# Moving one copy on ScalarE from step 7 to step 1 of the next batch, and writing a loop out

## The chip, the cores and the metric

The kernel runs on one core of a Trainium2 chip. The core has a matrix engine (TensorE, PE in the profile), a vector engine (VectorE, DVE), an activation engine (ScalarE, ACT), a general engine (GpSimd, POOL) and SyncE (SP), which here only issues DMAs. Each runs its own instruction stream; they meet only at semaphores. The metric is the device time of one execution in microseconds (us), the median of several.

## The reference, cut to what matters

The input is 8 images of 32x32 positions with 128 channels: 8 sequences of 1024 tokens. Three blocks follow each other.

```python
q = (x * dw1 @ pw1 + b1);  v = (x * dw2 @ pw2 + b2)          # per image, 1024 x 128
t = softmax(q @ q.T) @ v * gamma + x                         # attention inside an image
t = t + ssm(layernorm(t))                                    # conv, gated state-space scan
n = layernorm(t)                                             # the normed rows
probs = softmax(n @ router_w.T)                              # 8 experts
gates, experts = top_k(probs, 2)                             # a first and a second choice
out = t + sum(gate * expert(n) for both choices)
```

## The kernel before, in words

A **tile** is 128 tokens; there are 64, and a **batch** is the 8 tiles of one image (`NT` = 8). The program has two stages. In the first, which this change touches, all of attention, scan, norm and routing are done tile by tile, and every token's normed row is written to DRAM twice, once for each choice, into a region of its expert (`rows_by_expert`). In the second, 136 groups of 128 rows are fetched from there, run through their expert and written back; then the results are added and stored.

The first stage is a software pipeline written out by hand. Every engine has a function `step(base, i)` and runs it through `batches(eng, step)` (L191) 79 times: `base` is the first tile of a **round** (0, 8, 16, ..., 72) and `i` the step in it, 0 to 7. I number rounds by base / 8, so rounds 0 to 9. In step `i` of a round the engines work on several tiles at once: the scores of tile `base + i`, the rest of attention for the tile before it, the scan five and six tiles back, and the routing of the *batch before*, or of the one before that. The order in an engine's stream is the order of the lines of its `step`; what must wait for another engine does so by `upto(eng, semaphore, base, c)`. Rounds 0 and 1 are written out, rounds 2 to 6 are one loop with register `base` (`Fori`, L196), and rounds 7 to 9 are written out again. In the rounds of the loop a semaphore is compared with a value worked out in a register.

The path of one batch's normed rows, for the batch before round r:

- ScalarE, step 6 of round r (L657 to L665): writes the 8 normed tiles to `XA[:, 0]`, after it has waited for `scattered0`, the writes to DRAM of the previous content for the first choice.
- TensorE and ScalarE, step 7: `rows_of_x` (L303, L678) turns the rows, `logits` (L314) multiplies with the router.
- ScalarE, step 7 (L635 to L638): copies `XA[:, 0]` to `XA[:, 1]`, the rows for the second choice, in one instruction of 128x1024. It waits for `scattered1`: the eight writes of `XA[:, 1]`'s previous content. Behind it in ScalarE's stream stand `take_q` (L564, the next image's `QH`), the evacuation of the scan's projection (`XBC`, L646 and L648), and the first tap of the convolution (`CV`, L653). Who waits for them: `take_ql` on VectorE, the scores and the transposes `pY` (L334) on TensorE, and VectorE's convolution (L954).
- VectorE, step 1 of round r + 1: `route_a` (L889), the top two experts and gates, after a wait for `xa_copied`. Step 3: `route_b` (L923), the row numbers `SL`.
- GpSimd, steps 3 to 7 of round r + 1: one indirect DMA per tile and choice (`scatter_rows`, L863), issued at places named in the table `SPREAD` (L769). Rows 0 to 7 are the first choice, rows 8 to 15 the second; 8 to 11 stand in step 6 and 12 to 15 in step 7, at places 0 to 3. The last of them, row 15, is issued at place 3 of step 7.

In the last round (9) no tile is computed any more; its steps only route and write the last batch.

Of the kernel before, what the change touches and what calls it, by code (L numbers as in the profile page):

```python
# [5 lines left out]
def conv_attn_ssm_moe(nc, x, xT, dw1, pw1, b1, dw2, pw2, b2, gamma, w_zdt, w_xbc, conv_w, conv_b,  # L6
                      dt_bias, a_log, d_skip, gnorm_w, norm_w, w_outT, routerT, w1T, w3T, w2T, out):
    fp32, bf16, f32r = mybir.dt.float32, mybir.dt.bfloat16, mybir.dt.float32r
    ALU, ACT, AX = mybir.AluOpType, mybir.ActivationFunctionType, mybir.AxisListType
    P = 128  # L10
    TILES = x.shape[0] // P
    NT = 8
    SEQ = NT * P
    C = x.shape[1]
# [18 lines left out]
    with ctx:  # L33
        def sb(name, shape, dt=fp32):
            return ctx.enter_context(nc.sbuf_tensor(name, shape, dt))
# [4 lines left out]
        def sem(name):  # L40
            return ctx.enter_context(nc.semaphore(name))
# [61 lines left out]
        XA = sb("XA", [P, TOP, NT, ROW])  # L103
# [50 lines left out]
        def s(name):  # L154
            if name not in S:
                S[name] = sem(name)
            return S[name]

        def upto(eng, name, base, c):

            if not isinstance(base, int):
                eng.wait_ge(s(name), base + c)
            elif base + c > 0:
                eng.wait_ge(s(name), min(base + c, TILES))

        def apart(eng):

            eng.sem_inc(s("apart"), 1)

        class Steps:  # L170
# [5 lines left out]
            def then(self, ins, last=False):  # L176
                self.n += 1
                assert self.n < self.total
                if last:
                    ins.then_inc(self.sem, self.total - self.n + 1)  # L180
                    self.n = self.total
                else:
                    ins.then_inc(self.sem, 1)
                self.eng.wait_ge(self.sem, self.start + self.n)

        def there(base, c):
            return not isinstance(base, int) or 0 <= base + c < TILES
# [3 lines left out]
        def batches(eng, step):  # L191


            for i in range(2 * NT):
                step(i // NT * NT, i % NT)
            with eng.Fori(2 * NT, TILES - 2 * NT + 1, NT) as base:  # L196
                for i in range(NT):
                    step(base, i)
            for i in range(3 * NT - 1):
                step(TILES - NT + i // NT * NT, i % NT)  # L200

        NLOAD = 2 + 3 + 2 + 3 + 3 + 2 + 1 + 1

# [84 lines left out]
        def _(pe):  # L288
# [201 lines left out]
            project_q()  # L490
            pe.wait_ge(s("consts"), 1)
            batches(pe, step)


# [60 lines left out]
        def _(act):  # L555
            A = nc.scalar.activation
# [10 lines left out]
            def step(base, i):  # L567
# [63 lines left out]
                    last.then_inc(s("tr_ready"), 2)  # L631
                if i == 7 and there(base, -NT):
                    rows_of_x(base, 1)

                    upto(act, "xa_ready", base, 0)  # L635
                    if not (isinstance(base, int) and base == NT):
                        act.wait_ge(s("scattered1"), base * 16 - 16 * NT)
                    A(XA[:, 1, :, 0:C], XA[:, 0, :, 0:C], ACT.Copy).then_inc(s("xa_copied"), NT)  # L638
                if i == NT - 1 and there(base, NT):
                    upto(act, "qps", base, 2 * NT)  # L640
                    upto(act, "s_ready", base, NT)
# [32 lines left out]
                if i == 0 and there(base, -2 * NT):  # L674
                    upto(act, "lsub_ready", base, -NT)
                    A(PB[:], LG[:], ACT.Exp).then_inc(s("pexp_ready"), NT)

            def rows_of_x(base, grp):  # L678
                upto(act, "vT_ps", base, 4 * grp - 4)
                A(VT[:], pd[:], ACT.Copy).then_inc(s("vT_ready"), 4)  # L680
# [3 lines left out]
            act.wait_ge(s("loaded"), 16 * NLOAD)  # L684
            A(hrow[:, 1, :], hrow[:, 1, :], ACT.Exp).then_inc(s("a_exp"), 1)
            batches(act, step)

            def rows_T(n, par):
# [41 lines left out]
        def _(pool):  # L730
# [133 lines left out]

            pool.wait_ge(s("loaded"), 16 * NLOAD)
            batches(pool, step)

            def put(t, j):
# [9 lines left out]
        def _(dve):  # L878
# [10 lines left out]
            def route_a(base):  # L889

                bc = lambda a: a[:, :, None].broadcast_to([P, NT, E])
                steps = Steps(dve, "route_a_steps", base, -2 * NT, NT, 4)
                then = steps.then

                upto(dve, "xa_copied", base, -NT)
                v.tensor_copy(XA[:, 0, :, C + 1], TOK[:])
                ts(XA[:, 1, :, C + 1], TOK[:], float(TOKENS), None, ALU.add)
                upto(dve, "pexp_ready", base, -NT)
                then(v.tensor_reduce(r8[:, 1, :], PB[:], AX.X, ALU.add))
                then(v.reciprocal(r8[:, 2, :], r8[:, 1, :]))  # L900
                then(ts(TOK[:], TOK[:], float(NT * P), None, ALU.add))
                then(tt(PB[:], PB[:], bc(r8[:, 2, :]), ALU.mult))
                apart(dve)
                for j in range(NT):
                    last = v.max(M8[:, j, :], PB[:, j, :])
                then(last)
                apart(dve)
                for j in range(NT):
                    last = v.max_index(IX[:, j, :], M8[:, j, :], PB[:, j, :])
                then(last)  # L910
                then(tt(r8[:, 3, :], M8[:, :, 0], M8[:, :, 1], ALU.add))
                then(ts(r8[:, 4, :], r8[:, 3, :], 1e-9, None, ALU.add))
                then(v.reciprocal(r8[:, 5, :], r8[:, 4, :]))
                for c_ in range(TOP):
                    last = tt(XA[:, c_, :, C], M8[:, :, c_], r8[:, 5, :], ALU.mult)
                last.then_inc(s("xb_ready"), NT)
                then(v.tensor_copy(IXF[:], IX[:, :, 0:TOP]))
                for c_ in range(TOP):
                    last = tt(OH[:, c_], iota8[:, None, :].broadcast_to([P, NT, E]), bc(IXF[:, :, c_]), ALU.is_equal)
                then(last, True)  # L920
                tt(OHS[:], OH[:, 0], OH[:, 1], ALU.add).then_inc(s("onehot_ready"), NT)
# [17 lines left out]
            def step(base, i):  # L939
# [78 lines left out]
                if i == 1 and there(base, -2 * NT):  # L1018
                    route_a(base)
# [228 lines left out]
```

## Time and profile before

| | us |
|---|---|
| median of 3 runs | 1347.85 |
| lowest, highest | 1344.8, 1347.96 |
| the profiled execution | 1343.85 |
| its span (first to last instruction) | 1342.0 |
| first stage: until the first group's rows are fetched | about 978 |
| second stage | about 364 |
| one round of the loop | 111.2 |

The profile is of one execution. Its busy shares (TensorE 85%, VectorE 68%, ScalarE 51%, GpSimd 45%) are averages of both stages. The time between two rounds is best read from one event that every round has once: ScalarE's copy `V<-pX` (L669) in step 0, or VectorE's maximum over the scores `NM<-pX` (L980), which every step has once. In the timelines, "[3.73 <-DMA ...]" after a row is the time for which the engine sat idle before it, and what ended that; a row without it followed its predecessor at once.

### The profile page before, as it was taken

The numbers are of one execution on the slowest core, as the hardware profiler recorded it, in microseconds if no ns is written. First come the engines' busy times: TensorE is split into PE (matmuls) and PEld (weight loads), VectorE is DVE, ScalarE is ACT, GpSimd is POOL, SyncE is SP. The second block draws the span as 40 slices with busy tenths as digits, with TensorE's granted clock in tenths as the row PEclk, the third lists the DMA queues.
The fourth block names the chain that finished last, engine by engine and source line by source line (L and its number), as shares of the span: only waits on it lengthen the run. The fifth ranks groups of instructions, "written<-read, shape, count | busy, mean of one in ns | idle before, by whom it ended". The sixth has DMA issues, their size and how long they took to land.

```text
span 1342.0 us, 28912 instructions
## 1 busy us (share of the span) xinstructions
PE 1135.7 (85%) x7681; PEld 955.2 (71%) x7745; DVE 908.2 (68%) x3041; ACT 689.9 (51%) x1748; POOL 604.5 (45%) x846
## 2 busy tenths in 40 slices
PE   4799999998998998998999899774079999999950
PEld 3688888787877787877787787663058888888740
DVE  2578778867986886986898798672535555555535
ACT  2565675566565666566656666542034444444420
POOL 4133334573473465357347437436424444444430
PEclk9899999999999999999999999987579999999985
DMA  6000000100010010010001100000112222222239
GB/s 176 25 1 9 25 2 9 35 23 9 4 44 16 0 40 17 8 36 20 9 6 42 33 6 17 13 1 31 44 47 58 57 59 57 59 57 59 57 106 302
DMA packets 73005, 54.26 MB, mean 40 GB/s; under 512 B 9781, under 2 KB 67677, under 8 KB 72925
## 3 DMA queue, kind: packets, MB, share of 16 engines
q1 hardware_dynamic: 55437, 31.62, 8.7%
q0 software_dynamic: 8448, 17.45, 3.9%
q10 hardware_dynamic: 9040, 4.33, 1.1%
q8 instruction: 26, 0.43, 0.1%
q14 instruction: 54, 0.44, 0.1%
HBM read 30.67 MB, written 22.69 MB: 40 GB/s over the span
## 4 chain that ended last, share of the span: by engine, by line
PE 32%; DVE 19%; POOL 14%; issue 13%; DMA 4%; ACT 3%; DVEq 1%; SPq 1%; POOLq 0%; ACTq 0%
POOL rows_by_expert L863 7%; PE pX L512 6%; PE pY L514 6%; PE pd L529 3%; PE pb L529 3%; PE pc L521 3%; DVE CV L954 3%; PE pc L367 2%; DVE NM L980 1%; DMA rows_by_expert<-XA,SL 1%; POOL st L853 1%; PE pa L501 1%; PE pa L428 1%; DVE OFF L930 1%; POOL YG L810 1%
## 5 line engine op out<-in xcount | busy, mean ns | idle before, releaser
L872 POOL DMA_INDIRECT results_by_choice<-YE,DIX x136 | 130.2, 957 | 191.5 <-ACT YE L703 182.2
L863 POOL DMA_INDIRECT rows_by_expert<-XA,SL x128 | 139.5, 1090 | 64.1 <-issue 32.6
L1180 DVE COPY V<-pc 128x384 f32<-128x384 f32 x136 | 75.8, 558 | 133.3 <-PE pc L521 132.4
L367 PEld LDWEIGHTS pc<-XDT,M 128*128 128x128 f32 x1024 | 125.4, 196 | 35.9 <-issue 30.2
L367 PE MATMUL pc<-XDT,M 128*128 128x64 f32 x1024 | 126.3, 278 | 23.4 <-DVE CT L1085 9.8
L954 DVE SCALAR_TENSOR_TENSOR CV<-XBC,cw,CV 128x256 f32<-128x256 f32 x288 | 131.2, 491 | 20.7 <-issue 9.6
L428 PE MATMUL pa<-V,PT 128*128 128x128 f32 x1024 | 126.6, 277 | 2.2 <-POOL V L860 0.9
L428 PEld LDWEIGHTS pa<-V,PT 128*128 128x128 f32 x1024 | 119.4, 192 | 5.8 <-issue 5.3
L512 PE MATMUL pX<-W,TA 128*128 x272 | 104.7, 466 | 1.0 <-ACT TA L690 0.7
L810 POOL TENSOR_TENSOR YG<-Y,SZ 128x256 f32<-128x256 f32 x64 | 46.5, 727 | 123.0 <-DVE Y L1001 112.8
L514 PE MATMUL pY<-W,TA 128*128 x272 | 101.7, 456 | 0.0
L1045 DVE TENSOR_TENSOR M<-ED,GT 128x1024 f32<-128x1024 f32 x64 | 78.3, 1223 | 32.8 <-ACT ED L627 31.9
L801 POOL TENSOR_TENSOR STE<-ST,ETOT 32x256 f32<-32x256 f32 x56 | 46.5, 831 | 106.7 <-DVE ST L1102 102.6
L1176 DVE TENSOR_TENSOR X<-XT,pY 128x341 f32<-128x341 f32 x136 | 69.5, 511 | 31.7 <-PE pY L514 19.8
L980 DVE TENSOR_REDUCE NM<-pX 128x1 f32<-128x1024 f32 x64 | 77.9, 1217 | 14.2 <-PE pX L346 14.1
L334 PE MATMUL pY<-ident,PR 128*128 128x128 f32 x512 | 70.7, 283 | 19.5 <-ACT XBC L648 18.7
L673 ACT ACTIVATE TH<-CV 128x768 f32<-128x768 f32 x32 | 27.0, 844 | 112.3 <-issue 100.6
L334 PEld LDWEIGHTS pY<-ident,PR 128*128 128x128 f32 x512 | 59.7, 150 | 28.6 <-issue 15.2
L690 ACT ACTIVATE TA<-pa 128x128 f32<-128x128 f32 x136 | 37.7, 277 | 81.4 <-PE pa L501 80.6
L615 ACT ACTIVATE PR<-pX,NM 128x1024 f32<-128x1024 f32 x64 | 71.2, 1113 | 9.4 <-DVE NM L980 9.4
L521 PE MATMUL pc<-ident,X 128*128 128x128 f32 (+1 forms) x408 | 67.2, 274 | 0.0
L584 ACT ACTIVATE PT<-pY 128x1024 f32<-128x1024 f32 x64 | 64.4, 1006 | 3.8 <-PE pY L334 3.8
(252 smaller groups left out, 3022.0 us busy)
## 6 DMA issues: line engine op xcount, KB each, us to landing
GX<-rows_by_expert SPq DMA_DIRECT2D x136, 65.0 KB
XT<-in_xT_dram SPq DMA_DIRECT2D x8, 512.0 KB, 4.4
X<-in_x_dram SPq DMA_DIRECT2D x16, 256.0 KB, 2.9
W<-results_by_choice SPq DMA_DIRECT2D x8, 512.0 KB, 8.6
out_dram<-T ACTq DMA_DIRECT2D x8, 512.0 KB, 6.9
results_by_choice<-YE,DIX POOLq DMA_INDIRECT x136, 2.2
rows_by_expert<-XA,SL POOLq DMA_INDIRECT x128
W<-in_w1T_dram SPq DMA_DIRECT2D x1, 1364.0 KB
```

The source lines that it names most:

```text
L334: last = nc.tensor.transpose(pY[:, P * j:P * j + P], PR[:, P * j:P * j + P], ident[:])
L367: mm(pc[:, 64 * h:64 * h + 64], M[:, h, :], XDT[:, e % 2, HD * h:HD * h + 64], start=h == 0, stop=False, skip_group_check=True)
L428: last = mm(pa[:, 0:C], PT[:, P * j:P * j + P], V[:, j, :], start=j == 0, stop=j == NT - 1)
L512: mm(pX[:, 512 * par:512 * par + HID], GXT[:, par, :], W1[:, cols], start=True, stop=True).then_inc(s("h1_ps"), 1)
L514: mm(pY[:, 512 * par:512 * par + HID], GXT[:, par, :], W3[:, cols], start=True, stop=True).then_inc(s("h3_ps"), 1)
L521: last = nc.tensor.transpose(pc[0:hn, P * k:P * k + P], HH[:, par, h0:h0 + hn], ident[:])
L529: last = mm((pd, pb)[par][:, 0:C], HT[0:hn, par, k, :], W2[0:hn, bass.ds(expert, 1), k, :], start=k == 0, stop=k == len(HC) - 1)
L863: g.indirect_dma_start(xg, bass.IndirectOffsetOnAxis(ap=SL[:, j // NT, j % NT:j % NT + 1], axis=0), XA[:, j // NT, j % NT, :], None).then_ ...
L872: g.indirect_dma_start(yg, bass.IndirectOffsetOnAxis(ap=DIX[:, j, :], axis=0), YE[:, j, :], None).then_inc(s(f"ye{j}_scattered"), 16)
L954: return stt(CV[:, m, :], XBC[:, m, fo + tap:fo + tap + 256], cw[:, m, tap:tap + 1], CV[:, m, :], ALU.mult, ALU.add)
L980: v.tensor_reduce(NM[:, i:i + 1], pX[:], AX.X, ALU.max, negate=True).then_inc(s("nm_ready"), 1)
L1045: tt(M[:], ED[:], GT[:, None, :].broadcast_to([P, H, P]), ALU.mult).then_inc(s("m_ready"), 1)
```

## The change

The copy for the second choice leaves step 7 of ScalarE and stands at the end of step 1 of the next round. Its wait for `scattered1` asks for the same batch's writes as before (the base has grown by 8, so 8 tiles' worth is subtracted more). `route_a` on VectorE, which writes two columns of `XA[:, 1]`, waits for `scattered1` itself, in place of `xa_copied`. GpSimd still waits for `xa_copied` before row 0 in step 3. The table `SPREAD`, which puts the second choice's rows into steps 6 and 7, is the same in both files. `batches` becomes one written-out sequence of 79 steps on each of the four engines, so `base` is always a number.

```diff
         def batches(eng, step):
-            for i in range(2 * NT):
+            for i in range(TILES + 2 * NT - 1):
                 step(i // NT * NT, i % NT)
-            with eng.Fori(2 * NT, TILES - 2 * NT + 1, NT) as base:
-                for i in range(NT):
-                    step(base, i)
-            for i in range(3 * NT - 1):
-                step(TILES - NT + i // NT * NT, i % NT)
...
                 if i == 7 and there(base, -NT):
                     rows_of_x(base, 1)
-
-                    upto(act, "xa_ready", base, 0)
-                    if not (isinstance(base, int) and base == NT):
-                        act.wait_ge(s("scattered1"), base * 16 - 16 * NT)
-                    A(XA[:, 1, :, 0:C], XA[:, 0, :, 0:C], ACT.Copy).then_inc(s("xa_copied"), NT)
...
+                if i == 1 and there(base, -2 * NT):
+                    upto(act, "xa_ready", base, -NT)
+                    if not (isinstance(base, int) and base == 2 * NT):
+                        act.wait_ge(s("scattered1"), base * 16 - 32 * NT)
+                    A(XA[:, 1, :, 0:C], XA[:, 0, :, 0:C], ACT.Copy).then_inc(s("xa_copied"), NT)
...
-                upto(dve, "xa_copied", base, -NT)
+                if not (isinstance(base, int) and base == 2 * NT):
+                    dve.wait_ge(s("scattered1"), base * 16 - 32 * NT)
```

ScalarE, end of step 7 of a loop round and the first instructions of the next round, before (`VT` is the turned rows for the router, `QH` the next image's q, `PT` the transposed weights of the softmax, `TZ` the gate):

```order
L680 ACTIVATE VT<-pd 128x512 [waits vT_ps]
L638 ACTIVATE XA<-XA 128x8x128 [waits scattered1,xa_ready]
L162 REGISTER_ALU
L564 ACTIVATE QH<-pX,pcol 128x512 [waits s_ready,qps]
L564 ACTIVATE QH<-pX,pcol 128x512
L646 ACTIVATE XBC<-pc 128x2x256 [waits xbc01_ps]
L648 ACTIVATE XBC<-pY 128x256 [waits xbc2_ps]
L653 ACTIVATE CV<-XBC,cb,cw 128x256 [waits sx_ready,xbc2_evac]
L653 ACTIVATE CV<-XBC,cb,cw 128x256 x2
L196 REGISTER_ALU
L196 COMPARE_AND_BRANCH
```

The same place in the changed kernel (its lines have other numbers):

```order
L675 ACTIVATE VT<-pd 128x512 [waits vT_ps]
L559 ACTIVATE QH<-pX,pcol 128x512 [waits s_ready,qps]
L559 ACTIVATE QH<-pX,pcol 128x512
L636 ACTIVATE XBC<-pc 128x2x256 [waits xbc01_ps]
L638 ACTIVATE XBC<-pY 128x256 [waits xbc2_ps]
L643 ACTIVATE CV<-XBC,cb,cw 128x256 [waits sx_ready,xbc2_evac]
L643 ACTIVATE CV<-XBC,cb,cw 128x256 x2
L579 ACTIVATE PT<-pY 128x1024 [waits o_ps,pT_ps]
```

The copy and the branch are gone from there. ScalarE, end of step 1 and start of step 2 of the changed kernel:

```order
L636 ACTIVATE XBC<-pc 128x2x256 [waits xbc01_ps]
L638 ACTIVATE XBC<-pY 128x256 [waits xbc2_ps]
L643 ACTIVATE CV<-XBC,cb,cw 128x256 [waits sx_ready,xbc2_evac]
L643 ACTIVATE CV<-XBC,cb,cw 128x256 x2
L671 ACTIVATE XA<-XA 128x8x128 [waits scattered1,xa_ready]
L579 ACTIVATE PT<-pY 128x1024 [waits o_ps,pT_ps]
L595 ACTIVATE TZ<-pb 128x256 [waits sz_ready,z_ps]
L595 ACTIVATE TZ<-pd 128x256 [waits sz_ready,z_ps]
```

The copy now stands between the third convolution start and step 2's `PT`. VectorE, the end of a loop round and the start of the next one, before (`LG` the logits less their maximum, `CV` the convolution):

```order
L1102 TENSOR_TENSOR ST<-STE,pd 32x256 [waits ste_ready]
L1109 TENSOR_REDUCE r<-LG 128x8 [waits lg_ready]
L1111 TENSOR_TENSOR LG<-LG,r 128x64 [waits lmax_ready]
L196 REGISTER_ALU
L196 COMPARE_AND_BRANCH
L954 SCALAR_TENSOR_TENSOR CV<-XBC,cw,CV 128x256 [waits cv01_evac]
L954 SCALAR_TENSOR_TENSOR CV<-XBC,cw,CV 128x256
L954 SCALAR_TENSOR_TENSOR CV<-XBC,cw,CV 128x256 [waits cv_evac]
L980 TENSOR_REDUCE NM<-pX 128x1 [waits s_ready]
```

The same place in the changed kernel:

```order
L1098 TENSOR_TENSOR ST<-STE,pd 32x256 [waits ste_ready]
L1105 TENSOR_REDUCE r<-LG 128x8 [waits lg_ready]
L1107 TENSOR_TENSOR LG<-LG,r 128x64 [waits lmax_ready]
L950 SCALAR_TENSOR_TENSOR CV<-XBC,cw,CV 128x256 [waits cv01_evac]
L950 SCALAR_TENSOR_TENSOR CV<-XBC,cw,CV 128x256
L950 SCALAR_TENSOR_TENSOR CV<-XBC,cw,CV 128x256 [waits cv_evac]
```

The instructions that do work are the same and in the same order; the two that close the loop are gone.

## Rows read from the trace of the kernel before

**Rows 1.** Page, chain that ended last, share of the span by engine

```profile
PE 32%; DVE 19%; POOL 14%; issue 13%; DMA 4%; ACT 3%; DVEq 1%; SPq 1%; POOLq 0%; ACTq 0%
```

**Rows 2.** Waits: engine, line, waited for; us in total, times, longest

```profile
ACT XA L638 <- DMA rows_by_expert<-XA,SL: 25.2, 7, 4.0
```

**Rows 3.** Timeline, round 2 to 3: start us, us, engine, line, instruction

```profile
296.88 0.60 ACT L680 ACTIVATE VT<-pd 128x512 f32<-128x512 f32 x1 [0.55 <-PE pd L311]
298.80 0.96 POOL L863 DMA_INDIRECT rows_by_expert<-XA,SL  x1 [0.30 <-issue]
300.95 0.59 PE L472 MATMUL pd<-XW,BNAT 128*128 128x256 f32 x2
301.20 1.06 ACT L638 ACTIVATE XA<-XA 128x1024 f32<-128x1024 f32 x1 [3.73 <-DMA rows_by_expert<-XA,SL]
304.23 1.96 PE L334 MATMUL pY<-ident,PR 128*128 128x128 f32 x8 [2.68 <-ACT XBC L648]
305.80 0.62 DVE L1111 TENSOR_TENSOR LG<-LG,r 128x64 f32<-128x64 f32 x1
308.83 1.28 DVE L954 SCALAR_TENSOR_TENSOR CV<-XBC,cw,CV 128x256 f32<-128x256 f32 x3 [2.40 <-issue]
310.02 1.22 DVE L980 TENSOR_REDUCE NM<-pX 128x1 f32<-128x1024 f32 x1
```

**Rows 4.** Timeline, round 1 to 2, the entry into the loop

```profile
191.28 0.60 ACT L680 ACTIVATE VT<-pd 128x512 f32<-128x512 f32 x1 [0.54 <-PE pd L311]
191.78 1.05 ACT L638 ACTIVATE XA<-XA 128x1024 f32<-128x1024 f32 x1
195.79 1.04 PE L334 MATMUL pY<-ident,PR 128*128 128x128 f32 x8
198.78 1.22 DVE L980 TENSOR_REDUCE NM<-pX 128x1 f32<-128x1024 f32 x1
```

**Rows 5.** Timeline, round 6 to 7, the exit from the loop

```profile
741.76 0.60 ACT L680 ACTIVATE VT<-pd 128x512 f32<-128x512 f32 x1 [0.56 <-PE pd L311]
751.15 1.26 DVE L954 SCALAR_TENSOR_TENSOR CV<-XBC,cw,CV 128x256 f32<-128x256 f32 x3
752.34 1.21 DVE L980 TENSOR_REDUCE NM<-pX 128x1 f32<-128x1024 f32 x1
```

**Rows 6.** Timeline of ScalarE, step 0 to step 7, rounds 6 and 7

```profile
652.74 1.02 ACT L669 ACTIVATE V<-pX 128x1024 f32<-128x1024 f32 x1 [2.77 <-PE pX L300]
736.60 0.58 ACT L680 ACTIVATE VT<-pd 128x512 f32<-128x512 f32 x1
761.38 1.02 ACT L669 ACTIVATE V<-pX 128x1024 f32<-128x1024 f32 x1 [2.90 <-PE pX L300]
845.22 0.58 ACT L680 ACTIVATE VT<-pd 128x512 f32<-128x512 f32 x1
```

**Rows 7.** Timeline of TensorE, round 7 to 8

```profile
853.74 0.59 PE L472 MATMUL pd<-XW,BNAT 128*128 128x256 f32 x2
856.89 1.63 PE L334 MATMUL pY<-ident,PR 128*128 128x128 f32 x8 [2.55 <-ACT XBC L648]
```

**Rows 8.** Timeline of VectorE, round 8 to 9

```profile
941.37 0.23 DVE L1111 TENSOR_TENSOR LG<-LG,r 128x64 f32<-128x64 f32 x1
942.42 0.21 DVE L899 TENSOR_REDUCE r<-PB 128x8 f32<-128x64 f32 x1
```

**Rows 9.** Timeline of ScalarE, start of step 2 in round 2

```profile
223.47 1.00 ACT L584 ACTIVATE PT<-pY 128x1024 f32<-128x1024 f32 x1
225.03 0.38 ACT L600 ACTIVATE TZ<-pb 128x256 f32<-128x256 f32 x1 [0.55 <-PE pb L352]
225.75 0.38 ACT L600 ACTIVATE TZ<-pd 128x256 f32<-128x256 f32 x1 [0.34 <-PE pd L355]
```

**Rows 10.** DMA queues, 319 to 430 us: packets, MB, share of 16 engines

```profile
q14 instruction: 6, 0.05, 0.1%
```

**Rows 11.** DMA queues, 761 to 845 us, the same columns

```profile
q8 instruction: 5, 0.08, 0.5%
```

## The prediction

> **What bounds the kernel now.** I read the page first, then the waits, then timelines around the places that the waits name. The page's chain changes hands all the time: TensorE 32% of the span, VectorE 19%, GpSimd 14%, and 13% in which an engine waited for nothing the profile shows [rows 1]. So no engine is the bound; in the first stage the end is set by hand-overs, and a wait counts where it stands in that chain. Among the waits one belongs to the moved copy: ScalarE stood 25.2 us before it, in 7 rounds, until DMA writes of rows had landed [rows 2]. Those are rounds 2 to 8; round 1 has no earlier writes.
>
> The timeline of round 2 shows what that costs [rows 3]. ScalarE has the turned logit rows `VT` at 296.88 and then stands 3.73 us until the write issued at 298.80 has landed; the copy starts at 301.20 and takes 1.06. TensorE is through with its step at 301.5 (300.95 + 0.59) and stands 2.68 us until 304.23, for `XBC`, which is queued behind the copy. So this wait is on the path. Then a second hole: VectorE ends `LG` at 306.42 and starts the next round's `CV` only at 308.83, after 2.40 us marked issue, and the maximum `NM` of the new round follows at 310.02. From `VT` to `NM` it is 13.14 us.
>
> Two other boundaries show the same instructions without one or both holes. Round 1 to 2 has no writes to wait for: the copy starts at once at 191.78, the transposes at 195.79 without idle time, and from `VT` to `NM` it is 198.78 - 191.28 = 7.50 us [rows 4]. Round 6 to 7 has the writes but leaves the loop without jumping back: `CV` follows at 751.15 without idle time, and `VT` to `NM` is 752.34 - 741.76 = 10.58 us [rows 5]. So the wait for the writes costs 10.58 - 7.50 = 3.08 us, and the jump back costs 13.14 - 10.58 = 2.56 us, which is the 2.40 us hole and a little around it.
>
> **The change, part by part.**
>
> *The copy leaves step 7.* With it goes the wait. What is late next is known from round 1: there the copy itself (1.05 us) stood in ScalarE's stream and TensorE still ran on without idle time [rows 4], so the boundary is then TensorE's own row of products followed by VectorE's `LG` and `CV`. Taking out the copy's own 1.05 us therefore gives nothing in round 1, and nothing beyond the 7.50 us in the others. Rounds 2 to 6: 5 x 3.08 = 15.4 us. Round 7 computes no next image, so I read it from TensorE alone: its products end at 854.33 and the transposes start at 856.89, 2.55 us idle for `XBC` [rows 7]: 2.6 us. Round 8 has only routing left: VectorE's `LG` is done at 941.60 and `route_a`'s first sum starts at 942.42 [rows 8], with the end of the copy and the exponential between them. Without the copy in front of the exponential about 0.5 us of those 0.82 goes. Sum: 15.4 + 2.6 + 0.5 = 18.5 us.
>
> *The loop is written out.* The jump back is taken 4 times (rounds 2 to 3, 3 to 4, 4 to 5, 5 to 6): 4 x 2.56 = 10.2 us. Inside a round nothing is to be had: from `V` in step 0 to the first `VT` in step 7 the loop's round 6 takes 736.60 - 652.74 = 83.86 us and the written-out round 7 takes 845.22 - 761.38 = 83.84 us [rows 6]. The register arithmetic before the waits is hidden. The same pair bounds what straight code costs: round 7 runs it once and never again, and is no slower. Its price is more code to fetch: a loop round has 6 instruction packets on q14 and none on q8 [rows 10], the straight round has 5 on q8 in 84 us [rows 11]. I take 0 for it; what it costs if the cover is gone is a rival below.
>
> The Trainium skill (Advanced Engine Details and Errata, Control Flow Timing) gives a compare-and-branch about 108 ns. By that figure alone the four jumps would be worth 0.4 us and the whole change 18.9 us instead of 28.7. The trace does not agree with it as the whole cost of a jump: 2.40 us stand there on VectorE in the loop, none at the exit. The same page (ISA Cache) says that an engine's instruction cache holds two lines of 256 instructions, four times as much on TensorE, so a jump far back lands outside it; that would fit a jump that costs more than its own execution, but no row here shows it directly.
>
> *The copy arrives in step 1, in rounds 2 to 9.* It is 1.06 us on ScalarE, after the third `CV` and before step 2's `PT`. In round 2 `PT` starts at 223.47, ends at 224.47, and ScalarE then stands 0.55 us for TensorE before the first `TZ` and 0.34 us before the second at 225.75 [rows 9]. With the copy `PT` ends at 225.5, the first `TZ` starts at 225.5 instead of 225.03, and the second at about 225.8: the two holes, 0.89 us, swallow it but for some 0.1 us, and VectorE takes up `TZ` only after its `NM` of the step. `PT` itself is needed by products that stand at the end of TensorE's step. I take 0; the upper end is 8 x 1.06 = 8.5 us, the lower 0, since nothing leaves step 1. Its wait for the writes is over: the last write landed by 301.2, before the new round's first `NM`, and step 2 starts some 25 us after that `NM` (223.47 - 198.78 in round 2) [rows 3, 4, 9]. Behind the wait stand `PT` and `TZ`, should it not be.
>
> *The waits of the others.* VectorE's new wait for the same writes has the same answer. GpSimd waits for `xa_copied` in step 3, a full step after the copy. No DMA is added, removed or issued earlier in the order; the last writes of step 7 now overlap with products and transposes that before stood behind them. They touch nothing the engines use then.
>
> **The sum.** 18.5 + 10.2 = 28.7 us. The profiled execution took 1343.85 us (span 1342.0), so it would be 1315.2. The median of the runs shown, 1347.85, lies 4.0 above that execution; the same saving gives 1319.2, and that is what I forecast: **1319 us**.
>
> **The rivals.**
>
> *A: the hole at the jump does not go* (10%). The 2.40 us are marked issue, so the profile names no cause. If it belongs to the boundary and not to the jump, it stays; against that speaks the exit from the loop, with the same writes and no hole [rows 5]. It would leave 18.5 us: 1347.85 - 18.5 = 1329 us. By the Trainium skill's figure for a branch (Advanced Engine Details and Errata, Control Flow Timing) it would be 1329 us too.
>
> *B: something takes the wait's place* (8%). Round 1, my model, has no row writes on GpSimd in step 7, the others have. If they make the norm and state work late, each boundary gives back a part; half of the 15.4 is 7.7 us. The copy could also be on the path in step 1 after all, 8.5 us. Either alone: 1327 to 1328 us; both: 1335 us. Against it: up to `VT` and the products that follow, round 2 keeps round 1's pace: the last product starts 4.07 us after `VT` (300.95 - 296.88) and ends at 4.66, and in round 1 the transposes behind it start at 4.51 [rows 3, 4].
>
> *C: slower, because straight code has to be fetched* (4%). The mechanism: in rounds 2 to 6 TensorE's code came from its cache; now about 6 more packets a round come through q8. Their share, 0.5% of 16 DMA engines over 84 us, is 6.7 us or 1.3 us for one [rows 11]. If all 30 stood open they would cost 40 us, against a gain of 28.7: 1347.85 + 11 = 1359 us. It decides from some 22 of the 30 unhidden. Against it: round 7 fetches the same way and loses nothing [rows 6]. It would have to be that five such rounds in a row are unlike one.
>
> *D: more than forecast* (8%). Where TensorE has stood before, its next group is long: the eight transposes take 1.96 us at the jump and 1.63 us in round 7, against 1.04 in round 1 [rows 3, 4, 7]. In round 7 up to 0.6 us of that may come back, and later steps may gain a little likewise: up to 5 us in all, 1314 us.
>
> **How the numbers follow.** Forecast 70%, A 10%, B 8%, C 4%, D 8%. The forecast's own spread is small, about 4 us to each side, since the profiled execution and the median are 4 us apart. The range from 1312 to 1330 holds the forecast, A, D and the mild half of B. A measurement of this kernel can tell 0.3%, 4 us, from no change. Faster by more than that: forecast, A, B and D less 0.01 for a B far worse than priced, 0.95; C's 0.04 is split by how many fetches stand open: within 0.3% with the 0.01, 0.02; slower 0.03.
>
> **What would show it.** In the changed kernel's profile: no idle time of ScalarE before the copy; the copy in step 1 right after `CV`; `VT` to `NM` at about 7.5 us at every boundary of rounds 1 to 7 and no issue hole before `CV`; rounds of 105.5 us instead of 111.2; transposes of round 8 right after the products of round 7; about 30 more packets on q8. A hole before `CV` would mean A; 7.9 us or more between `VT` and `NM`, or a first `TZ` that VectorE waits for, B; idle time marked issue on TensorE in the middle of steps, C.

## The result, and the profile after

The changed kernel takes 1314.16 us in the median of 4 runs (1313.46 to 1316.24), the kernel before 1346.32 in 4 runs (1344.47 to 1347.96). The ratio is 0.9764, 95% interval 0.9744 to 0.9784: 31.8 us faster, with 29.1 to 34.5 as the ends of the interval. The forecast was 1319, a saving of 28.7. The profiled execution took 1313.46 us, its span is 1311.5 (1342.0 before).

Timeline of the changed kernel, round 2 to 3 (the place of [rows 3]), all engines, some rows:

```profile
295.58 0.60 ACT L675 ACTIVATE VT<-pd 128x512 f32<-128x512 f32 x1 [0.54 <-PE pd L306]
...
299.66 0.59 PE L467 MATMUL pd<-XW,BNAT 128*128 128x256 f32 x2
...
300.09 1.05 PE L329 MATMUL pY<-ident,PR 128*128 128x128 f32 x8
...
301.21 0.40 PE L340 MATMUL pX<-QL,QH 128*128 128x512 f32 x1
...
301.33 0.55 DVE L1107 TENSOR_TENSOR LG<-LG,r 128x64 f32<-128x64 f32 x1
...
301.80 1.27 DVE L950 SCALAR_TENSOR_TENSOR CV<-XBC,cw,CV 128x256 f32<-128x256 f32 x3
302.99 1.21 DVE L976 TENSOR_REDUCE NM<-pX 128x1 f32<-128x1024 f32 x1
```

Both holes are gone. The transposes start at 300.09 with no idle time named, in place of 2.68 us for `XBC`; `CV` follows `LG` at once, in place of 2.40 us of issue. From `VT` to `NM` it is 302.99 - 295.58 = 7.41 us instead of 13.14, and it is 7.41 at each boundary of rounds 2 to 6. The transposes take 1.05 us instead of 1.96.

ScalarE of the changed kernel, end of step 1 of round 2, where the copy now stands (compare [rows 9]):

```profile
220.79 0.59 ACT L643 ACTIVATE CV<-XBC,cb,cw 128x256 f32<-128x256 f32 x1
221.29 1.05 ACT L671 ACTIVATE XA<-XA 128x1024 f32<-128x1024 f32 x1
222.24 1.00 ACT L579 ACTIVATE PT<-pY 128x1024 f32<-128x1024 f32 x1
223.14 0.36 ACT L595 ACTIVATE TZ<-pb 128x256 f32<-128x256 f32 x1
224.14 0.38 ACT L595 ACTIVATE TZ<-pd 128x256 f32<-128x256 f32 x1 [0.64 <-PE pd L350]
```

The copy starts at once and `TZ` still waits for TensorE afterwards. Among the waits of the changed kernel none stands before the copy; the 25.2 us of [rows 2] are gone.

`V<-pX` in step 0 dates the rounds. The changed kernel, rounds 2 to 5:

```profile
205.89 1.03 ACT L659 ACTIVATE V<-pX 128x1024 f32<-128x1024 f32 x1 [2.66 <-PE pX L295]
...
312.03 1.02 ACT L659 ACTIVATE V<-pX 128x1024 f32<-128x1024 f32 x1 [2.67 <-PE pX L295]
...
417.48 1.02 ACT L659 ACTIVATE V<-pX 128x1024 f32<-128x1024 f32 x1 [2.67 <-PE pX L295]
...
523.48 1.02 ACT L659 ACTIVATE V<-pX 128x1024 f32<-128x1024 f32 x1 [2.67 <-PE pX L295]
```

A round takes 106.1, 105.5 and 106.0 us instead of 111.2. The whole difference of the spans, 30.5 us, lies as follows, worked out from such rows of both traces:

| stretch | saved, us | forecast |
|---|---|---|
| start, until the first `QH` (15.59 before, 13.65 after) | 1.9 | 0 |
| `V` of round 2 to `V` of round 7 (553.51, 529.01) | 24.5 | 25.6 |
| second `VT` of round 7 to that of round 8 (87.65, 84.34) | 3.3 | 2.6 |
| after that | 1.1 | 0.5 |

(`VT` is written in two halves; the second is the one shown at 295.58.) In the second line the forecast is 4 jumps and 5 waits, 4 x 2.56 + 5 x 3.08 = 25.6; 1.1 less was saved: the five boundaries gave 26.2, and the rounds between them lost 1.7 (below). The rows add to 30.8; the 0.3 left is above all the inside of round 7, from `V` to the second `VT`, where the change lost 0.4 us (89.36 against 88.99). The first line is not the change's: `before` issued its first loads at the same time, but its first products start at 11.77 us instead of 9.83, and every other kernel timed here has its first `QH` between 13.3 and 13.8. Less it, the two profiles differ by 28.6 us.

### The profile page after: what moved, and what is told of

The parts are those of the page before. It is cut to its first block and busy times, and to the rows that moved or that the text cites. A ratio compares the mean times of both kernels' runs of the same rounds, so it can differ in the third digit from the quotient of the medians.

```text
span 1311.5 us, 28238 instructions
## 1 busy us (share of the span) xinstructions
PE 1128.5 (86%) x7681; PEld 949.8 (72%) x7745; DVE 908.1 (69%) x3041; ACT 689.1 (53%) x1748; POOL 603.7 (46%) x846
## 5 line engine op out<-in xcount | busy, mean ns | idle before, releaser
L524 PEld LDWEIGHTS pb<-W,V 128*128 128x128 f32 (+1 forms) x408 | 56.1, 191 | 14.0 <-issue 1.1
```

What stands on the lines that cost most here:

```text
L524: last = mm((pd, pb)[par][:, 0:C], HT[0:hn, par, k, :], W2[0:hn, bass.ds(expert, 1), k, :], start=k == 0, stop=k == len(HC) - 1)
```

## The experiments

All eight timed kernels ran in two groups, each beside its own runs of the kernel before (7 in each; medians 1344.27 in the first group, 1343.22 in the second). Ratios are against those, with 95% intervals.

**One part alone.** `copy_only` moves the copy and leaves the loop standing, but over rounds 3 to 6 only, so with 3 jumps back and not 4 (in round 2 the new wait has no writes to ask for, and must know that when it is built). `unroll_only` writes the loop out and leaves the copy and its wait in step 7.

```diff
 copy_only, against the kernel before: the copy moved as in the change, and
-            for i in range(2 * NT):
+            for i in range(3 * NT):
                 step(i // NT * NT, i % NT)
-            with eng.Fori(2 * NT, TILES - 2 * NT + 1, NT) as base:
+            with eng.Fori(3 * NT, TILES - 2 * NT + 1, NT) as base:
 unroll_only, against the kernel before:
-            for i in range(2 * NT):
+            for i in range(TILES + 2 * NT - 1):
                 step(i // NT * NT, i % NT)
-            with eng.Fori(2 * NT, TILES - 2 * NT + 1, NT) as base:
-                for i in range(NT):
-                    step(base, i)
-            for i in range(3 * NT - 1):
-                step(TILES - NT + i // NT * NT, i % NT)
```

> The copy is moved to step 1 as in the change, but the loop stays, over rounds 3 to 6 (rounds 0 to 2 and 7 to 9 written out), so the jump back is taken 3 times instead of 4. My theory, two separate costs at a boundary: the wait goes (18.5 us) and one of four jumps goes (2.6 us): 21 us below before, about 1325 us, and 2.56 us too much at each of the three jumps, with a hole marked issue on VectorE before CV. The rival, that the hole before CV is a consequence of the stall on ScalarE and not of the jump: no hole at any boundary, and the time of the changed kernel, about 1314 us.

> The copy stays in step 7 with its wait; only the loop is written out. My theory: the four jumps go, 10.2 us below before, about 1336 us; ScalarE still stands 3.7 us before the copy in rounds 2 to 8. From VT to NM 10.6 us at every boundary of rounds 2 to 6. The rival, that the hole hangs on the stall: 2.4 us stay before CV and the time stays near before's, 1346 us. Inside the rounds: the changed kernel needed 89.0 to 89.7 us from V to the second VT where before had 89.0; if that is from straight code, it is here too; if it is from the copy in step 1, it is not.

Measured: `copy_only` 1323.97 us, ratio 0.9862 (0.9829 to 0.9896); `unroll_only` 1334.72 us, ratio 0.9927 (0.99 to 0.9954). By the ratios that is 18.6 us saved (14.0 to 23.0) and 9.8 (6.2 to 13.4), so each part is a gain alone; the two forecasts of a saving were 21 and 10.2. That `copy_only` came so near its forecast time of 1325 is in part luck: the saving was 2.4 us smaller, and the kernel before was faster in this group. The change has both parts. `copy_only`, round 3 to 4, VectorE's rows and TensorE's a few us later:

```profile
409.49 1.28 DVE L955 SCALAR_TENSOR_TENSOR CV<-XBC,cw,CV 128x256 f32<-128x256 f32 x3 [2.41 <-issue]
410.69 1.22 DVE L981 TENSOR_REDUCE NM<-pX 128x1 f32<-128x1024 f32 x1
...
415.21 0.43 PE L408 MATMUL pb<-ident,YG 128*128 128x128 f32 x2 [2.59 <-POOL YG L810]
415.48 3.17 PE L428 MATMUL pa<-V,PT 128*128 128x128 f32 x16
```

The hole at the jump stays, 2.41 us of issue, though the copy and its wait are gone. `VT` is at 400.71 there, so to `NM` it is 9.98 us, 2.57 above the change's 7.41: the jump's own price as forecast. But `V` comes at 421.38, 20.67 after `VT`, against 312.03 - 295.58 = 16.45 in the change: 4.2 us. The other 1.6 are TensorE's. It stood 2.59 us before 415.21, and its group of 16 products then took 3.17 us; the same group takes 1.95 us elsewhere in the kernel before (at 425.97). One stretch of `copy_only`, columns: us, then busy us and instructions of PE, PEld, DVE, ACT and POOL, then TensorE's granted clock as a share of the full one:

```profile
415.00:419.00 4.00, 3.79 (x21) 3.80 (x22) 3.68 (x15) 1.79 (x4) 1.50 (x4) 0.62 0.00 0
```

The clock was 0.62 there, so mostly at the lower of its two levels, 1.2 instead of 2.4 GHz. `unroll_only` has the mirror image, round 2 to 3:

```profile
299.56 1.06 ACT L633 ACTIVATE XA<-XA 128x1024 f32<-128x1024 f32 x1 [3.80 <-DMA rows_by_expert<-XA,SL]
...
302.68 1.94 PE L329 MATMUL pY<-ident,PR 128*128 128x128 f32 x8 [2.84 <-ACT XBC L643]
...
304.62 1.26 DVE L949 SCALAR_TENSOR_TENSOR CV<-XBC,cw,CV 128x256 f32<-128x256 f32 x3
...
304.84 0.63 PE L340 MATMUL pX<-QL,QH 128*128 128x512 f32 x1
```

The wait stands, the issue hole before `CV` is gone. TensorE stood 2.84 us, the transposes take 1.94 and a product of the scores 0.63, where the change shows 1.05 and 0.40. So the new round's `NM` is late too: from `VT` to `NM` it is 12.05, 11.21, 11.41, 10.81 and 11.22 us at the five boundaries, where I had expected 10.6 at each. TensorE's granted clock, and that of the kernel before and the change at the same place, in this order:

```profile
303.00:307.00 4.00, 4.00 (x15) 3.42 (x14) 2.79 (x9) 2.17 (x4) 0.61 (x1) 0.50 0.02 4
```

```profile
304.00:308.00 4.00, 3.77 (x14) 3.34 (x15) 2.32 (x7) 2.78 (x5) 0.61 (x1) 0.57 0.01 4
```

```profile
300.00:305.00 5.00, 5.00 (x37) 4.56 (x35) 4.60 (x13) 3.23 (x6) 0.61 (x1) 1.00 0.01 3
```

So in these three places, where TensorE had stood for 2.6 to 2.8 us, the products behind it ran at 0.50 to 0.62 of its clock; in the change it doesn't fall there. Two boundaries of one trace show what the clock alone does. In `dve_loop` (next experiment) TensorE stood 2.42 us before 415.11 and 2.35 us before 523.56, at two successive jumps without the wait, and ran its group of 16 products at a clock of 1.00 (415 to 419 us) and of 0.67 (524 to 528 us):

```profile
415.83 2.02 PE L432 MATMUL pa<-V,PT 128*128 128x128 f32 x16 [0.28 <-issue]
...
524.28 3.16 PE L432 MATMUL pa<-V,PT 128*128 128x128 f32 x16
```

From `VT` to `V` it is 19.42 us at the first and 20.48 at the second, 3.0 and 4.0 above the change: of the 4.2 us, the low clock is some 1.1, and standing alone did not bring it every time. What the other 0.4 us beyond the hole's 2.6 are is open. In the kernel before that slow stretch lay under VectorE's hole: much of TensorE's slow work ran while VectorE stood in a hole of its own. With one hole gone, the other brings its slow stretch onto the path; that reading fits the rows, but no run held the clock fixed. By the distance from `VT` to `V`, the two prices are (means over the five boundaries of the change and of `unroll_only`, the three jumps of `copy_only` and the four of the kernel before; `unroll_only` alone ranges from 19.85 to 22.18):

| `VT` to `V`, us | no wait | wait |
|---|---|---|
| no jump | 16.45 | 20.81 |
| jump | 20.63 | 22.21 |

The wait alone costs 4.4, the jump alone 4.2, both 5.8, not 8.5. My forecast split its 5.64 into 3.08 and 2.56; the total holds, since the change undoes both.

**Which engine's jump.** Both kernels have the moved copy. In `dve_straight` VectorE's stream is written out and TensorE, ScalarE and GpSimd loop over rounds 3 to 6; in `dve_loop` VectorE alone loops.

```diff
 dve_straight, in batches, before the loop of copy_only:
+            if eng in (nc.vector,):
+                for i in range(TILES + 2 * NT - 1):
+                    step(i // NT * NT, i % NT)
+                return
 dve_loop, there:
+            if eng in (nc.scalar, nc.gpsimd, nc.tensor,):
+                for i in range(TILES + 2 * NT - 1):
+                    step(i // NT * NT, i % NT)
+                return
```

> The changed kernel, but TensorE, ScalarE and GpSimd run a loop over rounds 3 to 6; VectorE alone is written out. If the jump costs time only on VectorE, the time is that of the changed kernel, 1314 to 1317 us. If the other engines' jumps count as well (before, the transposes took 1.96 instead of 1.04 us at a jump), 0.8 to 2.5 us more at each of 3 jumps: 1317 to 1322 us.

> The mirror image: VectorE alone runs the loop over rounds 3 to 6, the other three are written out. If VectorE's own jump is the cost: 3 x 2.56 = 7.7 us above the changed kernel, about 1322 us, with the hole before CV. If it takes all engines jumping at once (for instance if they share what brings the code): less than half of that, 1314 to 1318 us.

Measured: `dve_straight` 1313.48 us, ratio 0.9769 (0.9746 to 0.9793), as fast as the change; `dve_loop` 1328.79 us, ratio 0.9884 (0.986 to 0.9909). First two rows of `dve_straight`, then two of `dve_loop`, round 3 to 4:

```profile
399.31 0.60 ACT L684 ACTIVATE VT<-pd 128x512 f32<-128x512 f32 x1 [0.58 <-PE pd L315]
...
406.80 1.21 DVE L985 TENSOR_REDUCE NM<-pX 128x1 f32<-128x1024 f32 x1
```

```profile
409.63 1.28 DVE L959 SCALAR_TENSOR_TENSOR CV<-XBC,cw,CV 128x256 f32<-128x256 f32 x3 [2.58 <-issue]
410.82 1.22 DVE L985 TENSOR_REDUCE NM<-pX 128x1 f32<-128x1024 f32 x1
```

Three engines jump in `dve_straight` and `VT` to `NM` is 7.49 us; VectorE alone jumps in `dve_loop` (`VT` at 400.75) and it is 10.07. All of the jump's price is VectorE's. The expectation for `dve_loop` was too low by some 7 us: by `VT` to `V` its three jumps cost 3.0, 4.0 and 4.0 us, 11.1 and not 3 x 2.56 = 7.7, and its round 7 to 8 took 90.3 us, 5.9 more than the change's, in the profiled execution (below).

**Where the copy may stand.** `copy_twice` writes the same rows a second time to a scratch tile `XC` in step 1, in rounds 2 to 9. `copy_step2` puts the one copy into step 2, in front of `TH`. `copy_end7` puts it last in step 7, behind `QH`, `XBC` and `CV`. `changed_again` is the changed kernel itself, run beside them.

```diff
 copy_twice, against the change, ahead of the copy in step 1:
+                    if base > 2 * NT:
+                        act.wait_ge(s("extra"), base // NT - 2)
+                    for k_ in range(1):
+                        last = A(XC[:, k_], XA[:, 0, :, 0:C], ACT.Copy)
+                    last.then_inc(s("extra"), 1)
 copy_end7, against the change, last in ScalarE's step:
+                if i == 7 and there(base, -NT):
+                    upto(act, "xa_ready", base, 0)
+                    if not (isinstance(base, int) and base == NT):
+                        act.wait_ge(s("scattered1"), base * 16 - 16 * NT)
+                    A(XA[:, 1, :, 0:C], XA[:, 0, :, 0:C], ACT.Copy).then_inc(s("xa_copied"), NT)
-                if i == 1 and there(base, -2 * NT):
...
```

> The changed kernel itself once more, beside the variants of this call, since they differ from it by a few us at most. Expected 0.976 of before, within the first measurement's interval of 0.9744 to 0.9784.

> The changed kernel with a second copy of the same rows (into a scratch tile) in front of the first in step 1; it costs ScalarE 8 x 1.06 us more. If step 1 has the slack that I read from the two holes (0.89 us) and the one copy fits in, the second one must show: PT another 1.0 us later, the second TZ up to 1 us late, and 0 to 1 us a round, 0 to 8 us in all. The rival, that ScalarE in steps 1 and 2 is far from the path since VectorE's NM comes first: no change, under 2 us.

> The changed kernel with the copy in step 2, in front of TH, where ScalarE stood 5.3 us idle in every round. If the copy in step 1 costs anything (the excess of 0.1 to 0.7 us inside each round of the changed kernel), it comes back here, up to 2 us; if that excess is VectorE's straight code, as the run with only the loop written out says, the time is the changed kernel's within 1 us.

> The changed kernel with the copy back in step 7, but as ScalarE's last instruction there, behind QH, XBC and CV. What stalled before was what stood behind the waiting copy; the last write lands 4.3 us after VT and CV ends 6 us after VT, so the copy waits for nothing here. My theory: nearly all of the gain stays; PT of the next step 0 starts about 1 us later and TZ by up to 0.5 us, so 0 to 0.5 us for each of 5 boundaries, at most 3 us above the changed kernel. The rival, that the writes and the copy disturb the boundary by being there at all (contention): 5 us or more above.

| kernel | median, us | ratio | 95% interval |
|---|---|---|---|
| changed_again | 1314.80 | 0.9790 | 0.9767 to 0.9813 |
| copy_twice | 1316.23 | 0.9801 | 0.9776 to 0.9825 |
| copy_step2 | 1315.24 | 0.9791 | 0.9769 to 0.9814 |
| copy_end7 | 1315.15 | 0.9783 | 0.9760 to 0.9806 |

None can be told from the change. `changed_again` has the time of the change, 1314.80 for 1314.16 us, but its ratio of 0.9790 lies just outside the 0.9744 to 0.9784 that I had expected it in: the kernel before took 1343.22 us beside it and 1346.32 beside the first measurement. ScalarE of `copy_twice`, round 2, step 1 to 2:

```profile
221.13 1.05 ACT L675 ACTIVATE XC<-XA 128x1024 f32<-128x1024 f32 x1
222.09 1.04 ACT L677 ACTIVATE XA<-XA 128x1024 f32<-128x1024 f32 x1
223.03 1.00 ACT L580 ACTIVATE PT<-pY 128x1024 f32<-128x1024 f32 x1
223.94 0.36 ACT L596 ACTIVATE TZ<-pb 128x256 f32<-128x256 f32 x1
224.20 0.37 ACT L596 ACTIVATE TZ<-pd 128x256 f32<-128x256 f32 x1
```

The second copy uses up the rest of the holes before `TZ`, both of which are gone, and the rounds inside stay within 0.05 us of the change, but for one at 0.2. The second `TZ` comes at 224.20 where the change has 224.14; I had allowed it up to 1 us, so the two holes were not all the room there is, and of the two expectations it is the rival, under 2 us, that holds. Step 1 has room for two copies, and the 0 that I took for one is not luck. ScalarE of `copy_end7`, round 2 to 3:

```profile
297.21 1.27 ACT L559 ACTIVATE QH<-pX,pcol 128x512 fp32r<-128x512 f32 x2 [1.06 <-PE pX L289]
299.02 0.60 ACT L636 ACTIVATE XBC<-pc 128x512 f32<-128x512 f32 x1 [0.55 <-PE pc L450]
...
301.42 1.05 ACT L668 ACTIVATE XA<-XA 128x1024 f32<-128x1024 f32 x1
```

The copy is still in step 7 and its wait too, but by 301.42 the writes have landed, and no idle time stands before it. What cost time was neither the copy nor its step: it was that `QH`, `XBC` and `CV` were queued behind a waiting instruction. With these in front, the wait is over when it is reached.

**What makes VectorE's jump dear.** Two probes add, behind the last addition of the changed kernel, loops of 4 turns on VectorE whose bodies are n small copies (128x1) to a scratch tile. Each turn waits on a semaphore that the turn before raised. Nothing of the output is left out; the extra work makes the whole time long, and it is only the holes that are read.

```diff
+            dve.sem_inc(s("turned"), 1)
+            for k, n in enumerate((256, 320, 340, 360, 380, 400, 420)):
+                with dve.Fori(0, 4, 1) as turn:
+                    dve.wait_ge(s("turned"), turn + 4 * k + 1)
+                    for j in range(n):
+                        last = v.tensor_copy(probe[:, j:j + 1], pcol[:, 0:1])
+                    last.then_inc(s("turned"), 1)
```

`jump_probe` has the bodies 16, 64, 110, 150, 220, 300 and 420 in their place.

> The changed kernel with seven small loops on VectorE behind its last addition, each of 4 turns over a body of 16, 64, 110, 150, 220, 300 or 420 copies of 128x1; they touch only a scratch tile and run while the results are stored or after it. At each of 21 jumps the hole before the first copy of the next turn is read. VectorE's loop in the kernel before had 353 instructions and a hole of 2.4 us. Theory: the cost of a jump depends on how far back it goes; under 0.5 us for 16 and 64, about 2 us or more for 300 and 420, with a step in between. Rival: a jump costs VectorE 2.4 us whatever the body (then the probe shows it for 16 as well). Second rival: far jumps are cheap too and the 2.4 us belonged to the place (then no hole over 0.5 us anywhere).

> The same probe with bodies of 256, 320, 340, 360, 380, 400 and 420 copies. The first one had no hole up to 300 and one of 2.2 us, with a second of 1.5 to 1.8 us 11 copies later, at 420. If what counts is whether the whole body stays in what the engine holds of its code, there is one length between 300 and 420 from which every jump has a hole of 2.2 us, and below which none has, and VectorE's 353 instructions of the kernel before lie above it or within some tens of it (where a body starts may shift it). If instead the hole grows with the length, it is between 0 and 2.2 us for 340 to 400.

Measured: `jump_probe` 1638.45 us, with no hole at any jump of a body up to 300, where I had expected about 2 us at 300, and 2.2 to 2.3 us at each jump of the 420, with a second hole of 1.5 to 1.8 us 11 copies later. `jump_probe2` 1948.68 us: no hole at 256 and 320, one of 2.2 to 2.5 us at each jump from 340 on, and no second one at its 420. `jump_probe2`, a stretch of one turn of the 320 and one of the 340:

```profile
1392.05:1411.53 19.48, 0.00 (x0) 0.00 (x0) 19.45 (x323) 0.00 (x0) 0.00 (x0) 0.50 0.00 0
1494.36:1517.24 22.88, 0.00 (x0) 0.00 (x0) 20.66 (x343) 0.00 (x0) 0.00 (x0) 0.50 0.01 2
```

The first is busy for 19.45 of 19.48 us, the second has 2.2 us in which nothing runs. What ends the hole, on the timeline, and the DMA queues from 1517.3 to 1520.2:

```profile
1520.09 1.00 DVE L1209 COPY probe<-pcol 128x1 f32<-128x1 f32 x15 [2.22 <-issue]
```

```profile
q14 instruction: 1, 0.01, 1.1%
```

One packet of instructions arrives in the hole, and nothing else; the same queue has one packet in the hole of the kernel before (306 to 309 us), and none at a jump of the 320. So the engine jumps back to code that it no longer holds, and waits until it is fetched.

What it holds is not told by the length alone. A packet of this queue is 8 KB, and `dve_straight` tells how much code that is: from 410 us on VectorE alone runs straight code there, and between the first and the last of the eleven packets from 410 to 719 us VectorE's trace has 1283 instructions, waits on semaphores included: 128 for each of ten packets. The packets of that stretch, then those of the first turn of the 320 and of the 340 in `jump_probe2`:

```profile
q14 instruction: 11, 0.09, 0.1%
```

```profile
q14 instruction: 2, 0.02, 0.3%
```

```profile
q14 instruction: 3, 0.02, 0.5%
```

The code comes in pieces of 128, then, and the first turn of a body brings one packet for each new piece that it runs into: two for the 320, three for every body from 340 to 420, and four for the 420 of `jump_probe`, the one with the second hole, which starts at another place in a piece:

```profile
1552.63 24.84 DVE L1209 COPY probe<-pcol 128x1 f32<-128x1 f32 x409 [1.47 <-issue]
```

This second hole stands 11 copies behind the jump. In both probes the next packet starts some 0.5 us behind the first hole (1550.92 us here); a body that starts near the end of a piece wants that code before it is there, which is how I read the second hole. The other 420, like the 340, has none. So 340 and 420 cost the same, and 420 costs more at one start than at another: the start in a piece counts as well as the length. One end stays open: the 256 has three packets as well, the first right at its start and the last 0.06 us before its first branch, and no hole. The limit between 320 and 340 holds for these starts only; no other length than 420 was run at two. VectorE's loop in the kernel before is well beyond it: from branch to branch its trace has 515 instructions, 305 that work and 210 on registers, branches and semaphores, not the 353 of my expectations. ScalarE's has 273.

In the Trainium skill (Advanced Engine Details and Errata, ISA Cache) an engine holds two lines of 256 instructions. A loop of 515 is too long for that, as the trace agrees, but the probe does not agree with the size: the first turns of the 340 and the 360 run into six pieces in a row, so one of the two bodies would lie in no more than two lines of 256, and both have the hole at each jump.

## Why the prediction was right

*The two holes and what is late next: right.* Round 1 to 2 was the right model: 7.41 us at each boundary, forecast 7.50. Rival A is refuted (no issue before `CV`), and B too: the writes on GpSimd delay nothing by then, and the copy in step 1 is free, with room for another (`copy_twice`).

*The split into 3.08 and 2.56: wrong as prices, right as a sum.* The first came from a boundary without a jump against one without either, the second from subtraction, so that the sum is 13.14 - 7.50 whatever they are. Alone they are worth 4.4 and 4.2 at `V`. I read both off at `NM`, and so missed that TensorE, slow after having stood, is late with the next step's products. For the wait it shows at `NM` already: without jumps it cost 3.4 to 4.6 us there in `unroll_only`, not 3.08. Of the exit in the kernel before, round 6 to 7, `VT` to `V` is 19.62 us (761.38 - 741.76, [rows 5, 6]): 3.17 above 16.45, where the same wait in `unroll_only` costs 4.4 in the mean. Why the exit is milder is open.

*Straight code at no cost: a little wrong.* Round 2, VectorE's maxima of two steps, of the kernel before (loop) and of the change (straight):

```profile
251.31 1.21 DVE L980 TENSOR_REDUCE NM<-pX 128x1 f32<-128x1024 f32 x1
265.37 1.23 DVE L980 TENSOR_REDUCE NM<-pX 128x1 f32<-128x1024 f32 x1
```

```profile
249.71 1.20 DVE L976 TENSOR_REDUCE NM<-pX 128x1 f32<-128x1024 f32 x1
264.11 1.22 DVE L976 TENSOR_REDUCE NM<-pX 128x1 f32<-128x1024 f32 x1
```

The step takes 14.40 us instead of 14.06. There are such losses of about 0.35 us at a few fixed places, at the same ones when the change ran again; from `V` to `VT` rounds 2 to 7 lose 2.1 us in all (89.69, 89.0, 89.54, 89.4, 89.12 and 89.36, against 89.0). `unroll_only` and `dve_straight`, whose VectorE is straight too, have them, and in the rounds that VectorE loops in `copy_only` they are missing (88.7 to 89.1). That it is code fetched for VectorE fits this, and in the change a packet of q14 follows 0.7 us behind three such places (222.43, 252.18 and 468.03 us), but it was not measured by itself. So the rounds take 105.5 to 106.1 us and not 105.5 as I had put down. My comparison of rounds 6 and 7 in the kernel before [rows 6] was of two rounds that happened to agree. Of rival C, fetches on TensorE, there is nothing: q8 has 24 packets more than before, about the 30 forecast, and they cost nothing that the times show. The page of the change, then of the kernel before:

```profile
q8 instruction: 50, 0.82, 0.3%
```

```profile
q8 instruction: 26, 0.43, 0.1%
```

*Round 7 and the tail: right in direction, D's side.* 3.3 and 1.1 us for 2.6 and 0.5. The transposes of round 8 follow the products at once and take 1.05 us, so that the 0.6 us that D named did come back:

```profile
827.64 0.59 PE L467 MATMUL pd<-XW,BNAT 128*128 128x256 f32 x2
828.07 1.05 PE L329 MATMUL pY<-ident,PR 128*128 128x128 f32 x8
```

But this stretch is no good witness. From the second `VT` of round 7 to that of round 8 the kernels here without a wait before `QH` range from 82.5 to 90.3 us, and a low clock of TensorE goes with a long stretch. The change and `copy_end7`, one after the other:

```profile
846.00:868.00 22.00, 15.47 (x97) 12.25 (x98) 18.52 (x84) 11.97 (x31) 5.95 (x10) 0.89 0.00 0
```

```profile
846.00:868.00 22.00, 18.73 (x91) 14.86 (x92) 14.89 (x73) 9.85 (x27) 5.88 (x9) 0.71 0.00 0
```

At a clock of 0.71 the same 22 us hold 73 of VectorE's instructions instead of 84. `copy_end7` was profiled in an execution of 1319.94 us, 5 above its median. It is a spread of several us between single executions; none of the edits accounts for it (`dve_loop` has 90.3 us there and `copy_only` 82.5, with the same order of instructions).

*The level.* The forecast laid its saving on 1347.85, the median of three; a fourth run made it 1346.32. Of the 4.8 us between forecast and result, 1.5 are that, the other 3.3 the larger saving, which is less than two executions of one kernel often differ by. Beside `changed_again` the saving is 28.2 us by the ratio, and between the two profiles 28.6 without the late start, so nothing shows that the forecast's 28.7 was too small. The measured time is the 1314 of rival D, but D's reason is worth no more than its 0.6 us in round 7.

## What to carry to other kernels

Before moving an instruction that waits, ask what is queued behind it: putting it behind the others of its own step was worth as much here as moving it to another batch. Two holes of one boundary, each read by subtraction, give a reliable sum and unreliable parts, so predict the removal of both together and measure where the next event that everyone needs (`V` here, not `NM`) moves to. A loop whose code its engine does not hold in full pays at each jump, and its length is counted with all waits and register instructions, 515 here where 305 do work; the place to look is an idle time marked issue right behind the branch, with one instruction packet inside.

## What the runs showed of the hardware

- VectorE jumped back over bodies of up to 320 small copies with no hole and paid 2.2 to 2.5 us at each jump from 340 on. Its code came in packets of 8 KB, 128 instructions each, and a body of 420 had a second hole of 1.5 to 1.8 us at each jump from one start and none from another, so that the limit between 320 and 340 belongs to these starts. Jumps of the other engines cost nothing here (`dve_straight`); ScalarE's loop has 273 instructions.
- At three boundaries where TensorE had stood 2.6 to 2.8 us, its granted clock was 0.50 to 0.62 in the 4 us shown behind it, and the same products took 0.63 instead of 0.40 us. It is not a rule: at a jump of `dve_loop` TensorE stood 2.42 us and its clock stayed at 1.00, and the jump cost 3.0 us where the next two cost 4.0; before the transposes of round 7 in the kernel before it stood 2.55 us, and they took 1.63 us, in between [rows 7].
- Straight code on VectorE lost some 0.35 us at a few fixed places, 2.1 us over six rounds.
